# Eight-headed attention scores as stacked high/low fp32r products, full-row masks, and two layers' weights loaded in every pass

## The reference, cut to what matters

```python
xn = layernorm(x, ln_x_g, ln_x_b)            # x: the normalised context, 256 tokens
ln = layernorm(latents, ln_l_g, ln_l_b)      # latents: the stream x, 256 tokens
q = ln @ Wq                                  # 8 heads of 64
kv = jnp.concatenate([xn, ln], axis=1) @ Wkv # 512 keys
k, v = jnp.split(kv, 2, axis=-1)
sim = jnp.einsum('bhid,bhjd->bhij', q * scale, k) * scale
full_mask = jnp.concatenate([mask, jnp.ones((b, m), dtype=bool)], axis=1)
sim = jnp.where(full_mask[:, None, None, :], sim, max_neg)
attn = jax.nn.softmax(sim.astype(jnp.float32), axis=-1)
out = jnp.einsum('bhij,bhjd->bhid', attn, v) # then @ Wo and a layer norm
```

## Time and profile before

| | before |
|---|---|
| time, median of 3 runs | 5636.66 us (5631.06 to 5639.46) |
| profiled execution, own time | 5660.27 us |
| its span | 5658.5 us |
| PE busy | 4888.0 us, 86% |
| PE weight loads | 3477.8 us, 61% |
| DVE busy | 2758.3 us, 49% |
| ACT busy | 1853.5 us, 33% |
| mean granted TensorE clock | 0.921 |
| DMA | 218.95 MB |

### The profile page before, as it was taken

How to read it: one execution, slowest core, us unless ns; L and a number is a source line. 1 busy time by engine, 2 the same in 40 slices (tenths; PEclk the granted TensorE clock), 3 DMA queues, 4 the chain that set the end, 5 groups by cost and what they waited for, 6 DMA issues and landing times.

```text
span 5658.5 us, 74258 instructions
## 1 busy us (share of the span) xinstructions
PE 4888.0 (86%) x29184; PEld 3477.8 (61%) x29184; DVE 2758.3 (49%) x7346; ACT 1853.5 (33%) x3068; POOL 95.5 (2%) x180
## 2 busy tenths in 40 slices
PE   2898878989799897998979988899888998889988
PEld 1556765567656685565855658556585565855657
DVE  3535455354553545436454454544545445454454
ACT  2422324233242333423233242332424324242242
POOL 0000000000000000000000000000000000000000
PEclk9898989999899898998989989799897998989989
DMA  6000210002000020000200002000020000200002
GB/s 273 1 1 22 88 50 1 1 22 112 26 1 1 22 112 26 1 9 21 105 26 1 15 23 97 26 1 14 31 90 26 1 22 23 90 26 1 22 23 94
DMA packets 47155, 218.95 MB, mean 39 GB/s; under 512 B 4544, under 2 KB 16832, under 8 KB 27072
## 3 DMA queue, kind: packets, MB, share of 16 engines
q1 hardware_dynamic: 46784, 213.90, 10.2%
HBM read 192.91 MB, written 20.97 MB: 38 GB/s over the span
## 4 chain that ended last, share of the span: by engine, by line
PE 70%; DVE 19%; ACT 5%; issue 3%; DMA 2%; SPq 0%; POOL 0%; DVEq 0%; ACTq 0%
PE w L418 16%; PE w L428 10%; DVE mx L1023 6%; PE o L559 6%; PE w L675 6%; PE w L517 5%; PE w L667 4%; PE w L408 4%; PE w L531 4%; PE o L552 4%; PE w L484 2%; ACT oth L786 2%; PE w L534 1%; PE w L571 1%; PE w L467 1%
## 5 line engine op out<-in xcount | busy, mean ns | idle before, releaser
L824 ACT ACTIVATE pt<-w 128x1024 f32<-128x1024 f32 x640 | 653.8, 1024 | 768.6 <-PE w L534 440.4
L1023 DVE TENSOR_REDUCE mx<-w 128x4 f32<-128x1024 f32 x512 | 593.7, 1218 | 171.9 <-PE w L467 155.1
L559 PE MATMUL o<-pt,va 128*32 128x256 f32 x4096 | 559.5, 410 | 18.7 <-ACT pt L824 18.7
L786 ACT ACTIVATE oth<-w,res 128x256 f32<-128x256 f32 x656 | 264.1, 475 | 731.0 <-PE w L667 599.8
L1259 DVE TENSOR_REDUCE mx<-w 128x2 f32<-128x1024 f32 x128 | 156.9, 1226 | 527.0 <-PE w L519 527.0
L418 PE MATMUL w<-xnT,res 128*128 128x256 f32 x1408 | 375.3, 418 | 33.8 <-ACT xnT L778 24.5
L667 PE MATMUL w<-qsp,ksp 128*128 128x256 f32 x2048 | 350.3, 289 | 0.0
L418 PEld LDWEIGHTS w<-xnT,res 128*128 128x128 f32 x1408 | 281.3, 208 | 98.8 <-issue 47.6
L559 PEld LDWEIGHTS o<-pt,va 128*32 128x32 f32 x4096 | 207.9, 114 | 194.1 <-issue 67.8
L467 PE MATMUL w<-ksp,qsp 32*128 32x256 f32 (+1 forms) x2048 | 260.9, 401 | 73.5 <-DVE mx L1023 41.5
L418 PE MATMUL w<-xnT,stream 128*128 128x256 f32 x1280 | 311.8, 391 | 0.0
(11 more groups left out here) (235 smaller groups left out, 7506.6 us busy)
## 6 DMA issues: line engine op xcount, KB each, us to landing
stream_lo<-split SPq DMA_DIRECT2D x64, 1024.0 KB, 4.8
ksp<-split SPq DMA_DIRECT2D x64, 1024.0 KB, 6.9
stream<-in_moe_dram SPq DMA_DIRECT2D x80, 384.0 KB, 3.6
va<-in_moe_dram SPq DMA_DIRECT2D x8, 1024.0 KB, 10.3
split<-ksp SPq DMA_DIRECT2D x8, 1024.0 KB, 5.6
split<-qsp SPq DMA_DIRECT2D x8, 1024.0 KB, 8.0
res<-in_resident_dram SPq DMA_DIRECT2D x1, 8157.5 KB, 22.1
cx<-in_ctx_dram SPq DMA_DIRECT2D x16, 256.0 KB, 3.6
```

Source lines behind the costliest of these rows:

```text
L559: mm = pe.matmul(o[g:g + 32, 0:T], by_heads(plan, s)[:, kt, plan.v_of(h), :], pt[:, n % EXPS, a * 512 + kt * T:a * 512 + (kt + 1) * T], st ...
L786: h = act.activation(dst[:, c, :], w[:, c * T:(c + 1) * T], func, bias=bias[:, c:c + 1], **more)
L824: act.activation(pt[:, n % EXPS, :], w[:, :], ACT.Exp, scale=scale).then_inc(S["s_P"], 1)
L1023: dve.tensor_reduce(mx[s][:, :, 2 * u:2 * u + 2].rearrange("p t a -> p a t"), w[:, :].rearrange("p (a t k) -> p a t k", a=2, t=TT), AX_X, ...
```

## The change

Queries and keys of layer 1 are split into a high part rounded to fp32r and a low part, the f32 value minus the high part. A head has a chunk of `k1` of its own: its high part lies in its 64 rows and its low part in the other 64. `qsp` holds the high part of a head's queries in both row halves, and a second tile holds the low part in the head's rows and zero in the others. Two fp32r matmuls over 128 rows then give high x high + high x low, and low x high. For even heads the low queries lie in the memory of `kvT` (`hl`), for which `l1.q` moves behind `l1.kl` and `l1.vl` in the list; for odd heads in a new tile `qodd`. The mask products run over 128 rows, all but the first of them zero.

For the bigger `k1`, 4096 columns of layer 1's attention weights and 2048 of layer 3's first MLP matrix leave the resident tile. They are loaded into `stream` in each pass: layer 1's between `cx` and `x` at the head of the pass (2 MB), layer 3's after the last but one expert of layer 2 (1 MB). Layer 1's experts 0 to 4 now wait for the steps that read these weights in both slots.

```diff
-        + steps_of(s, "f0.add", "l1.ln", "l1.xT", "l1.q", "l1.kl", "l1.vl") + scores(L1, s) + values(L1, s)
+        + steps_of(s, "f0.add", "l1.ln", "l1.xT", "l1.kl", "l1.vl", "l1.q") + scores(L1, s) + values(L1, s)
...
+        W_["f3_w1"] = stream[:, 0:2048]
...
-        ksp, k1 = shared("ksp", [P, 8, T], F32R, "k1", [P, 4, L1_KEYS])
+        k1, ksp = shared("k1", [P, L1_HEADS, L1_KEYS], F32R, "ksp", [P, 8, T], F32R)
+        qodd = per_slot("qodd", [P, 4, T], F32R)
...
+        def q_low(s, h):
+
+            if h % 2 == 0:
+                return hl[s][:, :, :].rearrange("p a b -> p (a b)").rearrange("p (c t) -> p c t", t=T)[:, h // 2, :]
+            return qodd[s][:, h // 2, :]
...
@@ PE
                 if what in ("cT", "xT"):
                     w = take("l1." + what, s)
+                    pe.wait_ge(S["s_l1w"], 16)
...
-                        pe.matmul(w[:, tt * 512:(tt + 1) * 512], qz[s][:, u, tt * P:(tt + 1) * P],
-                                  k1[s][:, u // 2, :], start=True, stop=False)
-                        mm = pe.matmul(w[:, tt * 512:tt * 512 + T], ones_row[:, 0:P], maskb[s][:, :], start=False, stop=True)
+                        for n, q in enumerate((qsp[s][:, u, :], q_low(s, u))):
+                            pe.matmul(w[:, tt * 512:(tt + 1) * 512], q[:, tt * P:(tt + 1) * P], k1[s][:, u, :],
+                                      start=(n == 0), stop=False)
+                        mm = pe.matmul(w[:, tt * 512:tt * 512 + T], first_row[:, 0:P], maskb[s][:, :], start=False, stop=True)
...
-                        pe.matmul(o, k1[s][:, u // 2, kt * P:(kt + 1) * P], qz[s][:, u, :], start=True, stop=False)
+                        for n, q in enumerate((qsp[s][:, u, :], q_low(s, u))):
+                            pe.matmul(o, k1[s][:, u, kt * P:(kt + 1) * P], q, start=(n == 0), stop=False)
                         if kt < TT:
-                            pe.matmul(o, maskb[s][:, kt * P:(kt + 1) * P], ones_row[:, :], start=False, stop=False)
+                            pe.matmul(o, maskb[s][:, kt * P:(kt + 1) * P], first_row[:, :], start=False, stop=False)
...
@@ ACT
-                        for half in range(2):
-                            h = act.activation(qz[s][:, half::2, :], chunks_of(w, 4), ACT.Copy, scale=W_["half"][:, half:half + 1])
-                        h.then_inc(S["s_qz"], 1)
+                        for odd in range(2):
+                            for rows in range(2):
+                                h = act.activation(qsp[s][64 * rows:64 * rows + 64, odd::2, :],
+                                                   chunks_of(w, 4)[64 * odd:64 * odd + 64], ACT.Copy)
+                        h.then_inc(S["s_qhi"], 1)
                     elif step in ("l1.kc", "l1.kl"):
                         o = 0 if what == "kc" else T
-                        evac(k1[s][:, :, o:o + T], chunks_of(full(act, step, s), 4), "s_k1")
+                        w = full(act, step, s)
+                        for odd in range(2):
+                            r = slice(64 * odd, 64 * odd + 64)
+                            h = act.activation(k1[s][r, odd::2, o:o + T], chunks_of(w, 4)[r], ACT.Copy)
+                        h.then_inc(S["s_k1hi"], 1)
...
@@ DVE
+                    elif step == "l1.q":
+                        w = full(dve, step, s)[:, :].rearrange("p (c t) -> p c t", t=T)
+                        full(dve, "l1.vc", s)
+                        dve.memset(q_lows(s, 0)[64:128].bitcast(F32), 0.0)
+                        dve.wait_ge(*after("s_qhi", step, s))
+                        for odd in range(2):
+                            r = slice(64 * odd, 64 * odd + 64)
+                            h = dve.tensor_tensor(q_lows(s, odd)[r], w[r], qsp[s][r, odd::2, :].bitcast(F32), ALU.subtract)
+                        h.then_inc(S["s_qz"], 1)
+                    elif step in ("l1.kc", "l1.kl"):
+                        o = 0 if what == "kc" else T
+                        w = full(dve, step, s)[:, :].rearrange("p (c t) -> p c t", t=T)
+                        dve.wait_ge(*after("s_k1hi", step, s))
+                        for odd in range(2):
+                            r, other = slice(64 * odd, 64 * odd + 64), slice(64 - 64 * odd, 128 - 64 * odd)
+                            h = dve.tensor_tensor(k1[s][other, odd::2, o:o + T], w[r], k1[s][r, odd::2, o:o + T].bitcast(F32), ALU.subtract)
+                        h.then_inc(S["s_k1"], 1)
...
@@ DVE, once before the loop
-            dve.memset(ones_row[:, :], 1.0)
+            dve.memset(first_row[:, :], 0.0)
+            for s in range(SLOTS):
+                dve.memset(maskb[s][:, :], 0.0)
+                dve.memset(qodd[s][:, :, :].bitcast(F32), 0.0)
...
@@ SP
-            sp.dma_start(res[:, :], resident_in).then_inc(s_res, 16)
+            sp.dma_start(res[:, :], resident_in[:, 0:RESIDENT_COLS]).then_inc(s_res, 16)
...
                     sp.dma_start(cx[s][:, :, :], element(ctx_in, s).rearrange("o (t p) c -> p (o t) c", p=P)).then_inc(s_cx[s], 16)
+                sp.dma_start(stream[:, :], resident_in[:, RESIDENT_COLS:RESIDENT_COLS + LATE_COLS]).then_inc(S["s_l1w"], 16)
                 sp.wait_ge(s_out, 16 * SLOTS)
...
                     if e >= RING1:
                         used("f1.down", e - RING1)
+                    else:
+
+                        for name, steps in (("l1_wkv", ("l1.kc", "l1.vc", "l1.kl", "l1.vl")), ("l1_wq", ("l1.q",)), ("l1_wo", ("l1.out",))):
+                            if n * MOE1_COLS < late[name][1] and (n + 1) * MOE1_COLS > late[name][0]:
+                                for step in steps:
+                                    used(step, 0)
...
+                for e in range(MOE2 - RING2, MOE2):
+                    if e % RING2 == 0:
+                        used("f2.down", e)
+                sp.dma_start(stream[:, 0:2048], resident_in[:, RESIDENT_COLS + LATE_COLS:]).then_inc(S["s_f3w"], 16)
```

More of the change, by code:

```diff
@@ L47 @@
     ("cn_b1", 2), ("cn_b2", 1), ("cn_b3", 1), ("cn_b4", 1), ("gc_b1", 1), ("gc_b2", 1), ("gc_b3", 1), ("range", 1),
-    ("l1_wq", 1024), ("l1_wkv", 2048), ("l1_wo", 1024), ("lnx_g", 2), ("lnx_b", 2), ("lnl_g", 2), ("lnl_b", 2),
+    ("lnx_g", 2), ("lnx_b", 2), ("lnl_g", 2), ("lnl_b", 2),
     ("lno_g", 256), ("lno_b", 256), ("half", 2), ("sel3", 128),
@@ L55 @@
     ("l3_wq", 512), ("l3_wk", 512), ("l3_wv", 512), ("l3_bq", 2), ("l3_bk", 2), ("l3_bv", 256),
[1 row of a table removed]
[1 row of a table added]
 ]
+LATE = [("l1_wkv", 2048), ("l1_wq", 1024), ("l1_wo", 1024)]
+LAST = [("f3_w1", 2048)]
 RESIDENT_COLS = sum(n for _, n in RESIDENT)
+LATE_COLS = sum(n for _, n in LATE)
+RESIDENT = RESIDENT + LATE + LAST
 STAGE = [("sel8q", 256), ("sel8k", 256), ("sel16q", 256), ("sel16k", 256), ("sel1", 1024), ("f3_w2", 2048)]
@@ L238, in build @@
         at, W_ = 0, {}
-        for name, n in RESIDENT:
+        for name, n in RESIDENT[:-len(LATE + LAST)]:
             W_[name] = res[:, at:at + n]
@@ L254, in build @@
         onesf = sb("onesf", [P, P])
-        ones_row = sb("ones_row", [1, T], BF16)
+        first_row = sb("first_row", [P, T], BF16)
         def over(name, shape):
@@ L262, in build @@
         stream_lo = over("stream_lo", [P, STREAM_COLS])
+        W_["f3_w1"] = stream[:, 0:2048]
+        late, at = {}, 0
+        for name, n in LATE:
+            W_[name] = stream[:, at:at + n]
+            late[name] = (at, at + n)
+            at += n
         pt = sb("pt", [P, EXPS, 1024])
@@ L276, in per_slot, with shared @@
             return [sb(f"{name}{s}", shape, dt) for s in range(SLOTS)]
-        def shared(name, shape, dt, name2, shape2):
+        def shared(name, shape, dt, name2, shape2, dt2=F32):
             first, second = [], []
@@ L283, in shared @@
                 n = int(np.prod(shape[1:])) * 4
-                second.append(nc.alloc_sbuf_tensor_at(f"{name2}{s}", shape2, F32, offset=nc.sbuf_base - n))
+                second.append(nc.alloc_sbuf_tensor_at(f"{name2}{s}", shape2, dt2, offset=nc.sbuf_base - n))
             return first, second
@@ L291, in build @@
         mrow = per_slot("mrow", [1, T], U8)
-        maskb = per_slot("maskb", [1, T], BF16)
+        maskb = per_slot("maskb", [P, T], BF16)
         ctxT = per_slot("ctxT", [P, FC, T])
@@ L331, in build @@
         s_out = sem("s_out")
-        S = {n: sem(n) for n in (*COUNT, "s_wfull", "s_dve", "s_pool", "s_x0", "s_x1", "s_cx0", "s_cx1",
+        S = {n: sem(n) for n in (*COUNT, "s_l1w", "s_f3w", "s_wfull", "s_dve", "s_pool", "s_x0", "s_x1", "s_cx0", "s_cx1",
                                  *(f"s_moe1_{n}" for n in range(RING1)), *(f"s_moe2_{n}" for n in range(RING2)))}
@@ L362, in spread_views, with q_lows @@
             return to, frm
+        def q_low(s, h):
+            if h % 2 == 0:
+                return hl[s][:, :, :].rearrange("p a b -> p (a b)").rearrange("p (c t) -> p c t", t=T)[:, h // 2, :]
+            return qodd[s][:, h // 2, :]
+        def q_lows(s, odd):
+            if odd:
```

(9 more changed lines are left out.)

## The result

| | before | after |
|---|---|---|
| time, median of 4 runs | 5638.06 us (5631.06 to 5649.96) | 5693.57 us (5688.20 to 5700.17) |
| ratio to before | | 1.0097 [1.0076, 1.0117] |
| span of the profiled execution | 5658.5 us | 5692.3 us |

A forecast was written before the change was run, and what follows sets the result against it. PE was taken as the main bound (70% of the chain of waits). 8 x (-37.7 PE saving + 28.2 added waits + 5.0 clock) - 5 once = -41 us, so the median goes from 5636.7 to 5596, range 5530 to 5665.

The forecast's parts named there:

- the full-row mask's 0.11: Mask products of layer 1's scores on PE: priced at 0.11 us each, like the full-row bf16 product.
- `l0.oT.1`: Slot 1's out-transpose on PE, late behind context-key copies and subtractions that delay its norm: +4.3 us a pass.
- from slot 0's first exp to slot 1's first maximum: Layer 1's attention stretch between these two steps: forecast +0.4 us a pass.
- `l1.xT.0`: Slot 0's transpose on PE, late because DVE's turn, add and norm follow the context-key subtractions: +5.15 us a pass.
- the start of the loop: Before the passes: resident load 38% smaller, 8.5 us earlier, less 3 for memsets: -5 us once.
- the wait at the head: Start of each pass: x and mask issued behind 2 MB of weights, +4.7 us a pass, bounds 0 and 6.
- The second rival: Head of the pass: x is not held up by the 2 MB; 5558 us, chance 0.16.
- The clock: PE at its lower clock after five new waits and the head: 1 us each, +5 a pass, between 0 and 12.
- the first rival: Lower clock through slot 0's waits takes the gain: 12 us a pass, 5652 us; decides from 10 a pass; chance 0.24.
- what follows slot 1's wait: Slot 1's maxima with slot 0's last three exps: gain 15.0 us a pass; first rival: part (3.5) costs twice.
- slot 0's maxima: Layer 1, slot 0's maxima and the wait up to its first exp: gain 8.9 us a pass (7 to 11.4).
- The fp32r steps: Layer 1's scores on PE: maximum 1.12 us, gain 1.42; exp 1.60, gain 1.20; fp32r matmul of 512 columns 0.225.

The follow-up runs named there:

- run 6: Kernel before with only the change's per-pass loads of layer 1's attention weights and layer 3's matrix, scores unchanged: 5707.35 us, ratio 1.0112.
- run 2: Kernel before with only the mask products widened from one row to 128 rows: 5512.68 us, ratio 0.9766.
- run 10: Changed kernel with the mask products put back to one row: 5821.53 us, ratio 1.0304.
- runs 1 and 7: x and masks issued ahead of the 2 MB load: on the changed kernel, 5645.12 us; on the kernel before with only the change's loads, 5638.48 us.
- run 3: Changed kernel with thrown-away bf16 matmuls put on PE ahead of seven waits: 5617.52 us, ratio 0.9965.
- three mends: Changed kernel with x and masks ahead of the weights, another order of steps, and first maxima released by head parity: 5487.31 us, ratio 0.9732.

## Why the prediction was wrong, step by step

**The parts.** Loads +66 (run 6), masks -129 (run 2; 117 to 128 in run 10). If the parts add, the measured +55 leaves some +117 to the split of the scores. That is rough, since mending the order of the loads gave 66 us back on the kernel before and 48 on the changed one. The forecast had the masks inside one figure of PE work saved and never priced them by themselves: by its own rows they were 2 x 0.21 = 0.42 of the 1.20 saved on an exp, and they cost nothing elsewhere. In the table they alone bring 17 of a pass's 695.

**What held.** These steps came as forecast: the full-row mask's 0.11 (run 2); by the table `l0.oT.1` +4.4 for +4.3; from slot 0's first exp to slot 1's first maximum +0.4 for +0.4; `l1.xT.0`, in six of eight passes 13.3 before and 18.6 after, +5.3 for +5.15; the start of the loop 5.2 us earlier (99.32, now 94.15) for 5; the wait at the head +5.2 for +4.7. The rule of the Trainium skill that the forecast drew on ("DMA: Bandwidth & Descriptors", "Queues, rings and completion order": each engine consumes a ring's descriptors in their order) agrees with the trace: mask and `x` behind 2 MB came 6.2 us later, and runs 1 and 7 took that back. The second rival is dead.

**What failed: "The clock ... I charge 1 each ... +5".** Filling the waits, with the waits left in place, took 76 us back: 9.5 a pass by the medians, 11.5 by the two traces (700.3 to 688.8), of which the filled one is the fastest of its ten runs. So the clock's term was at least some 10 a pass, and not 5, and the point from which the first rival decides was reached.

The fills did not give back all. The granted clock is on record for every run, and 2 x (1 - clock) x span is its time at the lower level. In the median run that is 812 us before (20 runs beside run 3), 1127 after and 943 filled; the profiled execution of before, with its 895, took longer than any of these 20. So the change added some 315 us at the lower level, and the fills took away 184 of them for their 76 us, 0.41 us for each. Among the 20 runs of the unchanged kernel the time rises by 0.29 us for each us at the lower level. With these two rates 315 us cost 91 to 130 us, 11 to 16 a pass. That is an estimate; it lies around or above the upper end of the prediction's own bounds, 0 to 12.

The first rival named the mechanism, but only a part of the places. Of those it named, the queries (5.31 for 3.62) and `l0.oT` (1.09 for 0.66) were slow, and what follows slot 1's wait (in the table 3.5 of the forecast 15.0 are missing, 2.5 of which the fills give back). The keys (3.72) and `cT` (0.63) ran at full speed. And it did not name slot 0's maxima: there 2.9 of 8.9 are missing, and the fills give back 2.5. Its time was 5652, so it fell short of the measured one too.

Two reasons why I charged too little. I took the loss behind one wait in the trace of before (1.9), and then halved it because DVE would be the bound behind two of the waits. That holds for `l1.xT.0`, where PE's slow work ended 1.25 before DVE was done, but not for slot 0's maxima. And I charged the clock nothing behind the head: the loads by themselves cost 8.2 a pass by the medians, where the wait is 4.7 of them by the forecast and 5.6 by the table. The rest of layer 0 is 2.5 longer there and 3.5 in the changed kernel, within reach of its scatter from pass to pass.

How the filling gains is not all shown: it could in part take away low-clock time that was there before as well (the 5.40 of the earlier trace rows is such). That the filled kernel still has more time at the lower level than the one before (943 against 812) speaks against much of that; and the values of the earlier trace rows still take 5.89 in its first pass.

**Smaller.** The filled kernel gained 24 us on before by the medians, 2.4 a pass after the 5 once (6.3 by the traces, where the one of before is long for its kernel and the filled one short). The forecast without its clock term says 9.5, so 7.1 are missing. The clock that the fills did not mend accounts for some 5 of them by the estimate above (131 us x 0.29 = 38). The fp32r steps account for up to 2.6. From one exp to the next with values it is 0.06 (1.14 for 1.20). For an exp, its values and two maxima of slot 1, the traces have 10.09 before (344.93 to 355.02) and 6.31 filled (355.92 to 362.23), 3.78 for the 4.04 priced, which leaves 0.10 for a maximum; (0.06 + 0.10) x 16 = 2.6. The fp32r matmul of 512 columns, which I took at 0.225, measures 0.24 (374.83 to 375.07); the issue-gap rule of "TensorE: Matmul & The Clock Gate" of the Trainium skill ("Back-to-back issue gap"), 0.216, was low too.

**The level.** The forecast was made on a profiled execution 23.6 us above its median, and the changed kernel's stands at its median (5694.07, 5693.57). So the two traces differ by 34 us where the medians differ by 55, and the table above shows 9.7 us a pass of the miss (-9.5 + 5 forecast, +5.2 measured) where the medians show 12 (-41 and +55). The other 2.3 are lower clock in the trace of before (0.921, where the median run has 0.928), not a term of the change.

**What the split is worth.** With order and releases mended, the whole change takes 5487.3 (5479.4 to 5508.3), the masks alone 5512.7 (5507.7 to 5519.9), and their ratios' intervals overlap ([0.9708, 0.9756] and [0.9742, 0.9790]). So against the best that was tested, the fp32r scores themselves brought 25 us by the medians and 19 by the ratios, not clear of the noise, and that only after three mends; as the change places them they cost some 117. Masks together with the mends that don't need the split were not run, so it is open whether the split is worth anything. The three mends together gained 10 to 22 us more than singly; whether that is more than noise stays open too.

## What to carry to other kernels

Price a wait in front of PE twice: its length, and the matmuls behind it at the lower clock; here waits of 1 to 5 us cost at least some 10 us a pass beyond their length. Take the level from several runs: one profiled execution can hold 20 us of lower clock that the median does not. Work moved from PE to ACT and DVE pays when the steps queued behind it on those engines are not the ones that PE needs next, so change the order with the change, and issue what is needed first ahead of what is big. Split a change into its parts before pricing it: one edit of two tiles' shapes was here worth more (129 us) than all the rest with its mends (some 25).
